# Weight parts of Q, K and V kept in memory for the second batch entry; three smaller edits of order and waiting

## The reference, cut to what matters

```python
def attn(x, w, b, ow, ob):
    qkv = x @ w + b                       # w is (1024, 3072)
    q, k, v = ...                         # (B, 32, S, 32) each
    probs = softmax(einsum('bhqd,bhkd->bhqk', q, k) / sqrt(32))
    return merge(einsum('bhqk,bhkd->bhqd', probs, v)) @ ow + ob

def ffn(x):
    return (silu(x @ W_gate.T) * (x @ W_up.T)) @ W_down.T

x = x + attn(layernorm(x), ...)
x = x + ffn(layernorm(x))
```

## Time and profile before

| what | value |
|---|---|
| median of 3 runs | 3049.85 us (3049.22 to 3050.62) |
| the profiled execution's own time | 3051.18 us |
| its span in the profile | 3049.4 us |
| PE busy | 2984.3 us, 98% |
| DVE busy | 2314.5 us, 76% |
| ACT busy | 1663.0 us, 55% |
| POOL busy | 1173.3 us, 38% |
| DMA | 453.83 MB, mean 149 GB/s |

### The profile page before, as it was taken

How to read it: one execution, slowest core, us unless ns; L and a number is a source line. 1 busy time by engine, 2 the same in 40 slices (tenths; PEclk the granted TensorE clock), 3 DMA queues, 4 the chain that set the end, 5 groups by cost and what they waited for, 6 DMA issues and landing times.

```text
span 3049.4 us, 39070 instructions
## 1 busy us (share of the span) xinstructions
PE 2984.3 (98%) x13728; PEld 2341.1 (77%) x13728; DVE 2314.5 (76%) x3415; ACT 1663.0 (55%) x3039; POOL 1173.3 (38%) x848
## 2 busy tenths in 40 slices
PE   8999999998999999999999999999999999999999
PEld 7777777766777777776667878888878888888787
DVE  6899989898899898898897478866666666555653
ACT  2578778777788877777776143333333333332221
POOL 0234334333344343344342234444344444535730
PEclk9999999999999999999999999999999999999999
DMA  3334334343353534444744836532442223757874
GB/s 119 115 105 132 105 117 124 112 150 94 105 156 112 153 119 133 139 135 129 237 150 130 275 107 207 188 110 104 182 170 104 104 104 116 248 181 253 256 242 134
DMA packets 302211, 453.83 MB, mean 149 GB/s; under 512 B 31744, under 2 KB 175232, under 8 KB 292416
## 3 DMA queue, kind: packets, MB, share of 16 engines
q1 hardware_dynamic: 302016, 451.34, 46.8%
HBM read 306.00 MB, written 144.70 MB: 148 GB/s over the span
## 4 chain that ended last, share of the span: by engine, by line
PE 82%; DVE 13%; ACT 2%; issue 1%; DMA 1%; POOL 0%; SPq 0%; DVEq 0%; ACTq 0%
PE ps L874 19%; PE ps L875 19%; PE ps L876 19%; PE ps L946 6%; PE ps L965 6%; PE ps L977 6%; PE ps L982 6%; DVE mx L1327 4%; DVE pl L1349 4%; DVE wl L1299 1%; ACT ph L1107 1%; ACT pu L1106 1%; PE ps L907 0%; DVE xl L1293 0%; DVE bl L1412 0%
## 5 line engine op out<-in xcount | busy, mean ns | idle before, releaser
L1106 ACT ACTIVATE pu<-ps 128x512 f32<-128x512 f32 x1024 | 617.1, 603 | 327.8 <-PE ps L965 325.0
L1530 POOL TENSOR_TENSOR pl<-pu,ph 128x512 fp32r<-128x512 f32 x315 | 426.6, 1354 | 927.9 <-ACT ph L1107 927.4
L1327 DVE TENSOR_REDUCE mx<-ps 128x1 f32<-128x512 f32 x1024 | 696.9, 684 | 101.2 <-PE ps L946 91.5
L1107 ACT ACTIVATE ph<-ps 128x512 fp32r<-128x512 f32 x1024 | 615.8, 601 | 0.0
L1349 DVE TENSOR_TENSOR pl<-pu,ph 128x512 fp32r<-128x512 f32 x709 | 550.2, 777 | 54.0 <-ACT ph L1107 50.6
L874 PE MATMUL ps<-bh,gh 128*128 128x512 f32 x1208 | 471.7, 391 | 5.9 <-DVE bl L1412 2.5
L876 PE MATMUL ps<-bl,gh 128*128 128x512 f32 x1208 | 470.4, 389 | 0.0
L875 PE MATMUL ps<-bh,gl 128*128 128x512 f32 x1208 | 470.4, 389 | 0.0
L946 PE MATMUL ps<-kst,qst 96*128 96x512 f32 x1024 | 414.1, 404 | 17.2 <-DVE mx L1327 16.7
L965 PE MATMUL ps<-qst,kst 98*128 98x512 f32 x1024 | 408.6, 399 | 5.7 <-ACT ph L1107 3.1
L977 PE MATMUL ps<-ph,vt 128*65 128x512 f32 x1024 | 410.9, 401 | 0.6 <-ACT uu L1113 0.6
(11 more groups left out here) (142 smaller groups left out, 5250.3 us busy)
## 6 DMA issues: line engine op xcount, KB each, us to landing
graw<-in_wgu SPq DMA_DIRECT2D x42, 1024.0 KB, 5.1
sraw<-a_d SPq DMA_DIRECT2D x56, 704.0 KB, 5.0
wraw<-in_wqkv SPq DMA_DIRECT2D x24, 1024.0 KB, 5.4
qst<-q_d SPq DMA_DIRECT2D x192, 128.0 KB, 2.9
kst<-k_d SPq DMA_DIRECT2D x192, 128.0 KB, 3.1
a_d<-hs SPq DMA_DIRECT2D x88, 256.0 KB, 2.1
traw<-in_wd SPq DMA_DIRECT2D x77, 256.0 KB, 5.2
tt<-in_wd SPq DMA_DIRECT2D x77, 256.0 KB, 5.3
```

The source lines that it names most:

```text
L1106: e.activation(pu[sl][:, :], bk[:, :], ACT.Exp, scale=SCALE).then_inc(s["a_p"], 1)
L1107: e.activation(ph[sl][:, :], bk[:, :], ACT.Exp, scale=SCALE).then_inc(s["a_ph"], 1)
L1327: e.reduce_max(mx[:, j % 2, t, half:half + 1], ps[2 + bank_of["a", j, t, half]][:, :], AX.X).then_inc(s["v_mx"], 1)
L1530: e.tensor_tensor(pl[sl][:, :], pu[sl][:, :], ph[sl][:, :], ALU.subtract).then_inc(s["g_pl"], 1)
```

## The change

Four edits:

1. **Weights split once.** For batch 0 nothing of the split changes, but each quarter is written to memory after its `wlo`: a new step `wst`, two DMAs (`wh` and `wl`, 256 KB each) into `w_d`. For batch 1 (pieces 12 to 23) `wload`, `whi` and `wlo` are gone; instead a step `wpair` per quarter loads both parts back, two DMAs of 256 KB, at units 1, 5, 9 and 13. SP waits there for the stored piece (`d_wk`) and for PE's last product with the slot's previous piece. PE waits for the landing (`d_ws0`, `d_ws1`) in place of `v_wl`.
2. **Identity.** `idt` has its own semaphore `d_idt` and is issued right behind x tile 0, ahead of `wraw`; the bias is issued behind x tile 3.
3. **First product by quarters.** The first V product waits for one quarter of `wl` at a time, at its terms 0, 2, 4 and 6.
4. **Wo.** Of half 1 the last quarter's `wpart` moves from unit 11 to unit 17.

```diff
+    follow["wlo"] = lambda i, n: [(2, ("wst", i, n))]
...
             n = loads[0]
-            if n:
+            if 0 < n <= NW:
                 until("wlo", n - 1, 3)
-            step("wload", n)
-            for q in range(4) if n else ():
-                defer(5 + (4 if n > 3 else 1) * q, "whi", n, q)
+            if n < NW:
+                step("wload", n)
+                for q in range(4) if n else ():
+                    defer(5 + (4 if n > 3 else 1) * q, "whi", n, q)
+            else:
+                for q in range(4):
+                    defer(1 + 4 * q, "wpair", n, q)
             loads[0] += 1
+
+    def weighed(i):
+        until(*(("wlo", i, 3) if i < NW else ("wpair", i, 3)))
...
             for n in range(4):
-                defer(5 + 2 * n, "wpart", 1, n)
+                defer((5, 7, 9, 17)[n], "wpart", 1, n)
...
-                    pe.wait_ge("d_const", 32)
+                    pe.wait_ge("d_idt", 16)
...
-                        pe.wait_ge("v_wl", of_split(3 * g))
+                        if g or t:
+                            pe.wait_ge(*of_weights_of(3 * g))
...
+                    if g == 0 and t == 0 and k % 2 == 0:
+                        pe.wait_ge("v_wl", k // 2 + 1)
...
-                        pe.wait_ge("v_wl", of_split(u))
+                        pe.wait_ge(*of_weights_of(u))
...
-                    if t == 1:
-                        copy(idt[:, :], ident, "d_const")
+                    if t == 0:
+                        copy(idt[:, :], ident, "d_idt")
+                    elif t == 3:
                         copy(bqkv_c[:, :], bqkv, "d_const")
...
+                elif what == "wst":
+                    i, n = at_
+                    z = slice(2 * n, 2 * n + 2)
+                    sp.wait_ge("v_wl", i * 4 + n + 1)
+                    for part, src in enumerate((wh, wl)):
+                        copy(w_d[part, i, :, z, :], src[:, i % 2, z], f"d_wk{i % 2}")
+
+                elif what == "wpair":
+                    i, n = at_
+                    z = slice(2 * n, 2 * n + 2)
+                    sp.wait_ge(*of_kept(i - NW))
+                    sp.wait_ge(*of_kept(NW - 2 + i % 2))
+                    g, kind = divmod(i - 2, 3)
+                    if kind == 0:
+                        sp.wait_ge("p_v", of_v(g, TT - 1))
+                    else:
+                        sp.wait_ge("p_qk", of_qk(2 * g + 1, kind - 1, 1))
+                    for part, to in enumerate((wh, wl)):
+                        copy(to[:, i % 2, z], w_d[part, i - NW, :, z, :], f"d_ws{i % 2}")
```

More of the change, by code:

```diff
@@ L125, in v_group @@
         loaded(3 * g + 1)
-        until("wlo", 3 * g, 3)
+        weighed(3 * g)
         yield from past(g)
@@ L143, in qk_chunk @@
         loaded(i)
-        until("wlo", i, 3)
+        weighed(i)
         if c == B * KT - 1 and what == 1:
@@ L294, in schedule @@
         step("wlo", 0, q)
+        defer(2 + 2 * q, "wst", 0, q)
     transposed(0, 1)
@@ L571, in of_split, with of_weights_of, of_kept @@
     return 4 * (i + 1)
+def of_weights_of(i):
+    return ("v_wl", of_split(i)) if i < NW else (f"d_ws{i % 2}", 128 * ((i - NW) // 2 + 1))
+def of_kept(i):
+    return f"d_wk{i % 2}", 128 * (i // 2 + 1)
 def of_wh(i, n):
@@ L684, in wait_ge @@
             self.engine.wait_ge(self.sems[name], n)
-SEMS = ["d_const", "d_w", "g_wh", "a_wh", "v_wl", "p_tr", "a_xh", "v_xl", "v_st", "v_var", "a_sd", "v_rq", "v_n", "d_s", "v_ss",
+SEMS = ["d_const", "d_idt", "d_w", "g_wh", "a_wh", "v_wl", "p_tr", "a_xh", "v_xl", "v_st", "v_var", "a_sd", "v_rq", "v_n", "d_s", "v_ss",
         "p_v", "a_vh", "v_vl", "p_qk", "a_qh", "v_ql", "d_stg0", "d_stg1", "d_st0", "d_st1", "d_st2",
@@ L694 @@
 SEMS += [f"d_wo{half}{n}" for half in range(2) for n in range(2)]
-SEMS += ["d_bk"] + [f"d_b{q}" for q in range(7)] + [f"d_h{i}" for i in range(3)] + [f"d_yi{i}" for i in range(4)] + [f"d_n{t}" for t in range(TT)]
+SEMS += ["d_wk0", "d_wk1", "d_ws0", "d_ws1", "d_bk"] + [f"d_b{q}" for q in range(7)] + [f"d_h{i}" for i in range(3)] + [f"d_yi{i}" for i in range(4)] + [f"d_n{t}" for t in range(TT)]
 def program(nc, x, wqkv, bqkv, wo, bo, wgu, wt, wd, ident, out):
@@ L794, in program @@
         y_d = internal("y_d", (B, S, H))
+        w_d = internal("w_d", (2, NW, P, KT, 256))
         o_d = internal("o_d", (2, 2, P, KT, 512))
@@ L1090, in act_program @@
                     act.wait_ge("p_qk", n)
-                    act.wait_ge("d_const", 32)
+                    act.wait_ge("d_const", 16)
                     act.wait_ge("p_tr", of_tr(c // KT, TT - 1, 1))
@@ L1516, in pool_program @@
                     pool.wait_ge("d_w", 16 * (i + 1))
+                    pool.wait_ge(*of_kept(i - 2))
                     g, kind = divmod(i - 2, 3)
```

## The result

| | before | changed |
|---|---|---|
| median, us | 3050.23 (4 runs) | 3031.14 (4 runs, 3028.84 to 3035.70) |
| ratio | | 0.9939, 95% interval 0.9924 to 0.9954 |
| profiled execution, us | 3051.2 | 3028.8 (span 3026.8) |

What follows compares the result with a forecast made beforehand. Two nearly full engines, PE and DVE, coupled by two score banks, with DVE binding in places. 12 + 2.2 + 1.7 + 4.3 - 0.2 = 20.0 us off 3051.2 gives 3031.2, median 3030 us; range 3021 to 3044.

Steps and rivals of the forecast that it cites:

- weights, 760 to 1400: Batch 1's wl leaving DVE's queue from 760 to 1400 us: 12 us gained, taken between 8.6 and 17.9.
- weights and clock, 640 to 760: Waits at the first V product and one more shortened, 2.2 us; half clock behind the first avoided, 1.7 us or 0.
- Wo: Head 58's maxima land about 2.8 us sooner: wait of 2.63 us and half clock of 1.7 us go, 4.3 us together.
- start: First transposes and V product start sooner but DVE binds, and the identity delays x tile 1: a loss of 0.2 us.
- new DMAs on SP: 180 more DMAs, some 80 us of SP over the attention stage, covered by slack: priced at 0, 0 to 4 us for the range.
- more than its own time: Rival: without POOL's wh, DVE's pl is stretched less and backlogs shrink by more than wl; 28.7 us, 3021 us, chance 0.16.
- the next one takes its place: Rival: PE stalls on pl and mx anyway, so only plain waits count; 7.0 us, 3043 us, chance 0.16.
- Two signs: From 760 to 1400 us DVE's share near 84%; DVE's busy time down by some 46 us.
- the wait of 2.63 us goes: PE's wait for head 58's maxima, until 1512.68 us, vanishes once 1 MB of Wo's loads moves behind them.
- 64 KB, 0.2 us at the rate above, at most 0.5 us by the issue: At the start, the delay of x tile 1 by the identity's load now ahead of it.
- the slower rival: SP's queue holds the maxima in ten heads, 4.3 us each: 43 us less the 20 gained, 3073 us, chance 0.05.

Runs made afterwards that it cites:

- weights_only: Kernel before with only the weights' edit: batch 1's pairs come from DRAM, first loads, first product and Wo as before; 3035.74 us, ratio 0.9958.
- start_only: Kernel before with only the start's edits: identity ahead of the weights, bias behind x tile 3, first product by quarters; 3050.70 us, ratio 1.0008.
- wo_only: Kernel before with only the fourth quarter of Wo's second half moved from 11 to 17; 3045.38 us, ratio 0.9984.
- no_wo_move: Changed kernel with Wo's second half back at 5, 7, 9, 11; 3037.28 us, ratio to the kernel before 0.9959.
- dve_busy: Changed kernel with 48 unused instructions of wl's form put back into DVE's queue in batch 1; 3048.08 us, ratio to the kernel before 0.9993.
- both_busy: Changed kernel with 48 unused instructions of wl's form on DVE and 48 of wh's on POOL in batch 1; 3046.25 us, ratio to the kernel before 0.9987.
- pool_busy: Changed kernel with 48 unused instructions of wh's form put back into POOL's queue in batch 1; 3032.46 us, ratio to the kernel before 0.9944.
- pl_six: Changed kernel with first loads in the old order and six in place of five of a head's 16 pl on POOL; 3024.02 us, ratio 0.9915.

## Why the prediction was right, step by step

| term | predicted gain, us | trace of the changed kernel | by experiment |
|---|---|---|---|
| weights, 760 to 1400 | 12 | 11.1 | 10.8 (weights_only) |
| weights and clock, 640 to 760 | 2.2 + 1.7 | 4.2 | 4.0 (weights_only); 1.2 without the edit (start_only) |
| Wo | 4.3 | 3.2 | 3.5 (wo_only), 5.6 (against no_wo_move) |
| start | -0.2 | -1.2 | -1.2 (start_only), -0.2 (no_wo_move, dve_busy) |
| new DMAs on SP | 0 | 0 | 0.1 or less (both_busy) |
| sum | 20.0 | 18.1 at 2860 us | |

That the sum comes within 2 us is partly luck: the 12 us were a choice between 8.6 and 17.9 that nothing in the rows fixed, and the terms of the clock and of Wo rest on one execution each.

**Weights, 760 to 1400.** Right, and for the stated reason: DVE's queue carried the gain (dve_busy), and its size was set between PE's named waits (8.6 us) and the chain's share of `wl` (17.9 us), nearer to the lower. A plainer measure stood in the earlier trace rows unread: PE's idle time, 640 less 631.02, is 9.0 us. The gain is 7.7 us of it (1.3 are left), and 3.4 us in which the same matmuls count as busy for less time (631.0 us before; 640 less 11.1 less 1.3 is 627.6 now). The rival "more than its own time" had its mechanism partly right (DVE's `pl` 18 ns shorter) and its price wrong: there were not 18 us to be had. The rival "the next one takes its place" is out as well: the measured waits for `mx` and `mm` fell from 8.6 to 1.1 us. Two signs came out short. DVE's share there is 87% where 84% were expected, since more of the later work now falls into the stretch. Its busy time fell by 38 us where 46 were expected: the durations of `wl` did fall by 46 (88.4 to 42.0 us over the run), but they overlap their neighbours, and busy time counts an overlap once (all durations of DVE together fell by 52 us).

**640 to 760.** The wait at 704 was cut as foreseen, and the clock stayed up:

```profile
704.42 0.38 PE L895 MATMUL ps<-wh,xh 128*128 128x256 f32 x1 [1.61 <-DVE xl L1317]
```

```profile
704.00:708.00 4.00, 3.58 (x26) 3.29 (x27) 3.86 (x8) 1.09 (x2) 0.00 (x0) 1.00 0.42 130
```

against 2.47 us and 0.50. (Between the `wl` and the `xl` of the earlier trace rows stood two more short instructions of DVE, at 703.28 and 703.58 us.) But the half clock of the kernel before did not hang on the wait's length alone: wo_only waited 2.50 us there and fell, both_busy 2.49 us and did not.

```profile
707.06 0.38 PE L898 MATMUL ps<-wh,xh 128*128 128x256 f32 x1 [2.49 <-DVE xl L1320]
```

```profile
704.00:708.00 4.00, 1.51 (x10) 1.03 (x9) 3.96 (x7) 1.44 (x3) 1.37 (x2) 1.00 0.15 44
708.00:712.00 4.00, 4.00 (x28) 3.42 (x27) 3.37 (x7) 1.67 (x4) 0.00 (x0) 1.00 0.45 136
```

start_only, with all of the kernel before's work in this stretch, waited 2.47 us and did not fall either:

```profile
704.00:708.00 4.00, 2.26 (x16) 2.02 (x17) 3.83 (x9) 0.43 (x2) 0.05 (x1) 1.00 0.01 2
```

It gains 1.2 us from 640 to 760 (+1.2 to 0.0), as both_busy does. So of the 4.2 us some 1.2 are the clock's (predicted 1.7) and come from the execution that they were read from, and some 3.0 are the weights' (predicted 2.2).

**Wo.** Mis-sized in the sum. The step "the wait of 2.63 us goes" left 1 us standing:

```profile
1496.82 0.50 PE L989 MATMUL ps<-qst,kst 98*128 98x512 f32 x1 [0.96 <-DMA qst<-ml]
```

Half clock no longer follows it. Nor was 2.63 us a fixed quantity: it is the shortest of the four waits in traces without the move (2.63, 3.63, 3.87 and 4.49 us), where the six in which only the fourth quarter moved, with five `pl` a head on POOL, have 0.28 to 0.96 us. The term is too high by 1.1 us against the profiled execution of the kernel before, and too low against the other three, which lose 2.4 to 2.9 us from 1490 to 1600.

**Start.** The weakest step is "64 KB, 0.2 us at the rate above, at most 0.5 us by the issue". In the changed kernel x tile 1 slips by 1.0 us, twice that bound, and in both_busy by 2.4; in dve_busy, no_wo_move and pool_busy by 0.0 to 0.2, as predicted. The rows of before showed when the tile landed in one execution, and not how far that varies with one more transfer ahead of it. The rest held: the earlier transposes and products only wait for DVE's norm further on. In the changed kernel:

```profile
9.20 1.29 DVE L1266 BATCH_NORM_STATS2 st<-ln_x 128x6 f32<-128x512 f32 x2 [1.07 <-DMA ln_x<-in_x]
...
22.79 1.97 PE L928 MATMUL ps<-idt,ln_n 128*128 128x128 f32 x8 [3.52 <-DVE ln_n L1277]
```

**SP's queue.** The slower rival did not come: outside head 58 PE names no wait for `qst<-ml` up to 1500 us, and none for `w_d` at a product. In both_busy the whole traffic costs 0.1 us from 760 to 1400.

## What to carry to other kernels

Before a DVE instruction beside a nearly full PE is priced, read PE's idle time in that stretch: here the gain (11.1 us) lay near it (9.0), well below the chain's shares (17.9 for `wl` alone). A wait read from one profile is one draw: runs that leave its place untouched (here start_only) show how far it varies, and before two edits are said to act on each other, such a run must be looked at. The same goes for a load moved ahead of another at the start: three executions of six paid 0.2 us or less for it, three 1 us or more.

## What the runs showed of the hardware

- Executions of the same kernel differ: the kernel before ran from 3046.13 to 3054.67 us over all comparisons. In the thirteen traces much of the difference lies at the same few PE instructions. At one of the feed-forward stage (2865.07 us in the kernel before) PE stood still without a named releaser for 1.0 to 2.85 us in nine traces and not at all in four. Sums over instruction numbers, stretch by stretch, tell this from an edit, if runs that leave the place untouched are laid beside them.
- The length of PE's wait does not decide alone whether half clock follows. Ahead of the first V product of batch 1, it followed 2.47 us (the kernel before) and 2.50 (wo_only), but not 2.47 (start_only) and 2.49 (both_busy). At the wait for `xr` near 1675 us it followed 2.36 (wo_only) and 2.51 (both_busy), but not 2.39 (pool_busy) and 2.45 (pl_six). At the wait for `bl` at 1804.88 us, 2.32 to 2.36 us in all thirteen traces, it followed in two (start_only, no_wo_move), which lost some 1.5 us there.
- DMA traffic of 147 in place of 131 GB/s between 760 and 1400 us (both_busy against the earlier trace rows) left PE, DVE and POOL where they were.
